# A scan layer and mixture of experts on one core: a new order of every engine's list within a chunk, and of the transfers

## The chip, the core and the metric

The kernel runs on one core of a Trainium2 chip. A core has five engines that run their own lists in order: PE (matmuls; its weight loads are shown as PEld), DVE (vector), ACT (scalar), POOL (GpSimd) and SP, whose queue issues most DMAs here. They meet only through semaphores. The metric is the device time in microseconds; smaller is better.

## The reference

One layer of an adaptively modulated block, on x of 4 sequences x 2048 tokens x 256 channels, all in float32:

```
x = x + ga * attn(layernorm(x) * (1 + ca) + sa)
x = x + gb * moe (layernorm(x) * (1 + cb) + sb)

attn: xs, res = split(x @ in_proj.T)                  # 512 channels each
      xs = silu(causal conv of 4 taps(xs) + conv_b)
      dt, B, C = split(xs @ x_proj.T)                 # 64, 16, 16
      delta = softplus(dt @ dt_proj.T + b);  A = -exp(A_log)
      h = exp(delta * A) * h + delta * xs * B         # over the tokens, 512 x 16 states
      y = sum over the 16 states of h * C
      out = (y * silu(res)) @ out_proj.T
moe:  one shared expert for all tokens, and of seven others the best one for each token,
      each silu(b) * a with a, b = split(x @ w1), then @ w2
```

## The kernel before

The first of its two programs does the attention, the shared expert and the routing; the second gathers tokens for the seven other experts. The change touches only tables of the first.

The 8192 tokens are 16 chunks of 512, four to a sequence. In a chunk the 512 x 16 states are 16 **sets** of 32 channels, a set has 4 **groups** of 4 states, and a group is one tile of 128 partitions x 512 tokens. (s, g) is group g of set s; 64 scans make a chunk. Each set s passes through these steps:

- SP copies delta of 32 channels to four blocks of partitions (transfer `D` s). ACT makes dA = exp(delta * a) for each group (`exps`, L850) into three banks of PSUM, so it can be three scans ahead of DVE.
- The input delta * xs is spread over the partitions, for ten sets by PE (`spread_u`, L580, called U here) and then multiplied by B on DVE (L960, a load of a set into the ring of 8 sets), for the six sets 2, 5, 7, 10, 13 and 15 by a DMA (transfer `U` s) and multiplied by B on POOL (`IN` s, L1272).
- DVE scans the four groups (L973). ACT saves the last column as the state (`save`, L865); the save of set s-1 stands just ahead of dA (s, 3) in ACT's list.
- POOL multiplies the set by C (`weigh_states`, L1279, the weighing), PE adds up the states of four sets (`SUM` j, L590, sets 4j to 4j+3), and DVE multiplies that by the gate (L982). Only when SUM j is made may a set take the ring's places that its sets held.

Between these stand the items of the rest of the layer. Their **names**: `T`, `XS`, `RS`, `CV`, `XP`, `DT`, `DB` are the front of a later chunk (turning, input projection, convolution, x_proj, delta and its linear branch), `OP` the output projection, `T2`, `RB`, `GL`, `GT`, `B`, `A`, `Y` the shared expert of an earlier chunk (turned norm, rows back for the routing, logits, logits turned, the two halves of w1, w2). `LN`, `LN2` are layer norms on DVE, `R`, `R2` their reciprocal roots on POOL, `N`, `N2` the normalizing on ACT, `G`, `G0`, `GM`, `RC` the shared expert's gate, `DU` delta * xs on POOL, `L0`, `L1` the logarithms, `SU` and `SRS` the silus with the loads of their tables (L753, L757, L761, L764), `HALO` three columns of the convolution. An item carries an offset: ("XS", 0), 1 in chunk c works for chunk c+1.

What **sets the order** are tables: `plan[s]` lists what PE does in set s after its U, `evict[s][g]` what ACT does after dA (s, g), `vector[s][g]` what DVE does after scan (s, g), `gps[s]` what POOL does after the weighing of set s, and `transfers` SP's list for a chunk. Each list is followed strictly in order, and an item blocks all behind it on its engine until its semaphores are there. Items that ACT evicts from PSUM share two banks in turn, items that DVE reads (SUM, OP, DB, A, Y) share one; `take_bank` makes PE wait until the item before in the bank is evicted. Chunks 0, 1, 14 and 15 are written out, the others are four to a round of a loop.

Of the kernel before, what the change touches and what calls it, by code (L numbers as in the profile page):

```python
# [102 lines left out]
def fused_program(nc, ins, t, bc_dram, wout_dram, w2_dram, mod_dram, gb_dram, rows_dram, logits_dram):  # L103
# [5 lines left out]
    with ExitStack() as ctx:  # L109
# [78 lines left out]
        plan = {
            0: [(('Y', 1), -2), (('XS', 0), 1), (('XS', 1), 1), (('DB', 2), 0), (('XS', 2), 1), (('DB', 3), 0), (('XS', 3), 1)],
            1: [],  # L190
            2: [(('SUM', 3), -1)],
            3: [(('CV', 0), 1), (('CV', 1), 1)],
            4: [],
            5: [(('OP', 0), -1), (('CV', 2), 1), (('CV', 3), 1), (('OP', 1), -1), (('RS', 0), 1), (('RS', 1), 1), (('SUM', 0), 0), (('XP', 0), 1)],
            6: [],
            7: [],
            8: [(('RS', 2), 1), (('RS', 3), 1), (('T2', 0), -1), (('T2', 1), -1), (('DT', 0), 1), (('DT', 1), 1), (('RB', 0), -1)],
            9: [(('GL', 0), -1), (('RB', 1), -1), (('SUM', 1), 0), (('GT', 0), -1), (('B', 0), -1), (('B', 1), -1), (('B', 2), -1), (('DB', 0), 1), (('B', 3), -1), (('DT', 2), 1)],
            10: [],
            11: [(('DB', 1), 1), (('DT', 3), 1), (('A', 0), -1)],  # L200
            12: [(('T', 0), 2), (('SUM', 2), 0), (('T', 1), 2)],
            13: [(('A', 1), -1), (('A', 2), -1)],
            14: [(('A', 3), -1)],
            15: [(('Y', 0), -1)]}
        evict = {
# [16 lines left out]
        vector = {  # L222
            0: [[(('Y', 1), -2)], [], [(('DB', 2), 0)], []],
            1: [[], [(('DB', 3), 0)], [], []],
            2: [[], [], [], []],
            3: [[(('SUM', 3), -1)], [], [], []],
            4: [[], [], [], [(('OP', 0), -1)]],
            5: [[], [], [], [(('OP', 1), -1)]],
            6: [[(('LN2', 0), -1)], [], [], []],
            7: [[], [(('SUM', 0), 0)], [], []],  # L230
            8: [[], [], [], []],
            9: [[], [], [], []],
            10: [[], [(('SUM', 1), 0), (('LN', 0), 2)], [], []],
            11: [[], [], [(('DB', 0), 1)], []],
            12: [[(('DB', 1), 1)], [], [], [(('A', 0), -1), (('RC', 0), -1)]],
            13: [[], [], [(('SUM', 2), 0)], []],
            14: [[(('RC', 1), -1), (('A', 1), -1)], [], [(('A', 2), -1)], []],
            15: [[(('A', 3), -1)], [], [], [(('Y', 0), -1)]]}
        gps = {
            0: [(('DU', 1), 0), (('IN', 5), 0)],  # L240
            1: [],
            2: [],
            3: [(('IN', 7), 0)],
            4: [(('R2', 0), -1)],
            5: [(('IN', 10), 0)],
            6: [],
            7: [],
            8: [(('IN', 13), 0), (('R', 0), 2), (('G0', 0), -1)],
            9: [],
            10: [],  # L250
            11: [(('IN', 15), 0), (('DU', 0), 1)],
            12: [],
            13: [],
            14: [(('IN', 2), 1)],
            15: []}
# [1365 lines left out]
```

How the kernel before makes its waits and increments, by code:

```python
def hold(eng, sem, value, held):  # L63
    eng.wait_ge(sem, value)
    eng.sem_inc(held, 1)
# [235 lines left out]
        def take_bank(pe, g, c, f):  # L303
            at = (c, g, f) if known(c) else (2, g, 2 + off_of_item[g])
            if at in before:
                x, b = before[at]
                pe.wait_ge(kept[x[0]], many[x[0]] * (b if known(c) else c + (b - 2)) + x[1] + 1)
            return banks[bank_of[g]]
# [1 line left out]
        def read_bank(eng, g, f):  # L311
            eng.wait_ge(made[g[0]], many[g[0]] * f + g[1] + 1)
            return banks[bank_of[g]]
# [22 lines left out]
            def keep_bc(f):  # L336
                sp.wait_ge(xdbl_ready, f + 1)
                sp.dma_start(bc_dram, xdbl[DT_ROWS:PROJ, :]).then_inc(bc_kept, 16)
# [7 lines left out]
            def spread_bc(f, par):  # L346
                keep_bc(f)
                hold(sp, bc_kept, 16 * f + 16, held)
                if known(f) and f == 1:
                    sp.wait_ge(scaled, 2 * BATCH)
                if not known(f) or f >= 2:
                    sp.wait_ge(dbu_own, N_OWN * (f - 1))
                    sp.wait_ge(dbu_shared, N_SHARED * (f - 1))
                load_rep(b_rep, 0, par, b_loaded)
                if not known(f) or f >= 2:
                    sp.wait_ge(hc_ready, NSET * (f - 1))
                load_rep(c_rep, 1, par, crep_loaded)
# [72 lines left out]
            def body(c, m):  # L431
# [5 lines left out]
                    transfer(kind, n, c, m)  # L437
                    if known(c) and c == 0 and kind == "X":
                        sp.wait_ge(ga_stored, 16)
                        load_w_out(0)
```

## Time and profile before

| | us |
|---|---|
| median of 3 runs | 2424.81 (2423.86 to 2426.68) |
| profiled execution | 2425.52 |
| its span, first to last instruction | 2423.7 |
| its mean granted clock of TensorE | 0.917 of 2.4 GHz |
| POOL's first step of the root `R` in four chunks in a row | 1051.67, 1167.04, 1283.50, 1399.13 |

The chunks take the span's first 1890 us; then come the last routing and the experts. In the profile a busy time is the time in which an engine runs instructions; idle time stands in brackets ahead of an instruction, with the engine and line that ended it. A chunk here is counted from one `R` to the next, so it begins in set 9 of one chunk and ends in set 8 of the following. The first chunk of a sequence scans without a start state, and each such scan is a little shorter.

### The profile page before, as it was taken

What the parts mean: (1) busy time and instruction counts of PE and PEld (TensorE: products, weight loads), DVE (VectorE), ACT (ScalarE), POOL (GpSimd) and SP (SyncE); (2) the same over time, 40 slices, a digit from 0 to 9 for tenths busy, and PEclk for the clock granted to TensorE, in tenths of its full rate; (3) what the DMA queues carried; (4) which work ended last, traced back from release to release, by engine and by line L of the source; (5) the groups of instructions that cost most, each with busy time, mean ns of one, the idle gap of its engine ahead of it and who ended that gap; (6) DMA issues with size and microseconds to landing.
All of it is one profiled execution on the core that took longest, in us unless ns stands there. A gap on an engine that the chain in (4) does not pass through costs nothing. (4 is left out here: it accounts for less than half of the span.)

```text
span 2423.7 us, 31216 instructions
## 1 busy us (share of the span) xinstructions
PE 2129.3 (88%) x7668; PEld 1007.6 (42%) x7669; DVE 1948.4 (80%) x2114; ACT 1346.9 (56%) x2391; POOL 1979.4 (82%) x858
## 2 busy tenths in 40 slices
...
GB/s 175 137 101 98 78 106 65 104 74 117 77 102 72 98 74 103 83 101 103 75 111 74 108 68 117 80 103 69 98 69 53 208 42 87 86 87 85 84 85 47
DMA packets 148360, 224.35 MB, mean 93 GB/s; under 512 B 47187, under 2 KB 84577, under 8 KB 144098
## 3 DMA queue, kind: packets, MB, share of 16 engines
...
q14 instruction: 109, 0.89, 0.1%
...
## 5 line engine op out<-in xcount | busy, mean ns | idle before, releaser
L1279 POOL TENSOR_TENSOR ring<-ring,reps 128x2048 f32<-128x2048 f32 x256 | 1154.7, 4530 | 42.6 <-ACT state L865 42.6
L973 DVE TENSOR_TENSOR_SCAN ring<-dA,state,ring 128x512 f32<-128x512 f32 x768 | 929.7, 1262 | 13.5 <-ACT dA L850 9.2
L850 ACT ACTIVATE dA<-d_rep,a 128x512 f32<-128x512 f32 x1024 | 690.1, 686 | 433.1 <-DVE ring L973 426.4
L1272 POOL TENSOR_TENSOR ring<-u_rep,reps 128x2048 f32<-128x2048 f32 x96 | 436.2, 4544 | 44.6 <-PE bank L590 44.5
L960 DVE TENSOR_TENSOR ring<-u_ps,reps 128x2048 f32<-128x2048 f32 x160 | 360.5, 2269 | 8.8 <-issue 4.9
L590 PE MATMUL bank<-ring,spread 128*32 128x512 f32 x2048 | 283.2, 703 | 42.4 <-POOL ring L1279 37.8
L561 PE MATMUL bank<-n,w1s 128*128 128x512 f32 x512 | 266.1, 657 | 61.1 <-DVE delta L941 38.5
L973 DVE TENSOR_TENSOR_SCAN ring<-dA,ring 128x512 f32<-128x512 f32 x256 | 293.7, 1201 | 11.5 <-ACT dA L850 10.4
L1553 DVE TENSOR_TENSOR hid<-z,sg 128x512 f32<-128x512 f32 x70 | 48.4, 692 | 295.6 <-ACT sg L1530 295.6
L1468 PE MATMUL z<-ring,hT 128*128 x560 | 262.2, 612 | 3.6 <-issue 2.1
L516 PE MATMUL bank<-xin,w_in 128*128 128x512 f32 x512 | 244.9, 619 | 8.3 <-ACT xin L701 8.3
L520 PE MATMUL bank<-xpad,w_conv 128*128 128x512 f32 x496 | 224.0, 601 | 8.9 <-ACT us L716 8.8
L527 PE MATMUL bank<-xdbl,w_dt 65*128 65x512 f32 x256 | 149.0, 680 | 68.9 <-ACT n L732 52.1
...
L561 PEld LDWEIGHTS bank<-n,w1s 128*128 128x128 f32 x512 | 98.2, 205 | 195.6 <-issue 93.2
L590 PEld LDWEIGHTS bank<-ring,spread 128*32 128x32 f32 x2048 | 69.9, 127 | 233.4 <-issue 213.2
L580 PE MATMUL u_ps<-us,spread 32*128 32x512 f32 x320 | 161.6, 705 | 0.0
L516 PEld LDWEIGHTS bank<-xin,w_in 128*128 128x128 f32 x512 | 99.6, 198 | 131.9 <-issue 119.2
L1468 PEld LDWEIGHTS z<-ring,hT 128*128 128x128 f32 x560 | 101.9, 192 | 122.4 <-issue 122.3
L1530 ACT ACTIVATE sg<-z 128x512 f32<-128x512 f32 x70 | 41.8, 597 | 199.5 <-PE z L1468 199.5
L520 PEld LDWEIGHTS bank<-xpad,w_conv 128*128 128x128 f32 x496 | 92.1, 190 | 132.5 <-issue 110.8
L1486 PE MATMUL y_ps<-reps,hidT 128*128 x560 | 132.4, 379 | 0.8 <-ACT hidT L1519 0.8
...
## 6 DMA issues: line engine op xcount, KB each, us to landing
d_rep<-delta SPq DMA_DIRECT2D x1024, 64.0 KB, 2.0
reps<-bc_rows SPq DMA_DIRECT2D x128, 256.0 KB, 6.3
u_rep<-us SPq DMA_DIRECT2D x384, 64.0 KB, 2.0
...
```

Of the source, the lines that this page charges most:

```text
L516: last = nc.tensor.matmul(ps_[:, :], t["w_in"][:, k, col:col + P], hT[:, k, :], start=(k == 0), stop=(k == KD - 1))
L520: last = nc.tensor.matmul(ps_[:, :], t["w_conv"][:, j, k, :], xpad[:, j, k:k + T], start=(k == 0), stop=(k == KCONV - 1))
L527: last = nc.tensor.matmul(ps_[:, :], t["w_dt"][:, j * P:(j + 1) * P], xdbl[0:DT_ROWS, :], start=True, stop=True)
L561: last = nc.tensor.matmul(ps_[:, :], t["w1s"][:, k, col:col + P], h2T[:, k, :], start=(k == 0), stop=(k == KD - 1))
L580: nc.tensor.matmul(u_ps[:, i % 2, :], t["spread"][DS * q:DS * q + DS].rearrange("p f d -> p (f d)"), us[DS * q:DS * q + DS, par, j, :], st ...
L590: last = nc.tensor.matmul(ps_[DS * q:DS * q + DS, :], t["gather"], hs[:, (SPC * j + q) % RING, n, :], start=(n == 0), stop=(n == NG - 1), ...
L850: nc.scalar.activation(dA[:, u % ABANK, :], d_rep[:, q, :], ACT.Exp, scale=t["a"][:, u:u + 1]).then_inc(da_ready, 1)
L960: nc.vector.tensor_tensor(hs[:, s % RING], u_ps[:, i % 2, :].unsqueeze(1).to_broadcast([P, NG, T]), b_rep[:, par, :].rearrange("p (g t) -> ...
L973: nc.vector.tensor_tensor_scan(hs[:, s % RING, g, :], dA[:, u % ABANK, :], hs[:, s % RING, g, :], state[:, u:u + 1] if m else 0.0, ALU.mul ...
L1272: nc.gpsimd.tensor_tensor(hs[:, s % RING], u_rep[:, i % UBUF, :].unsqueeze(1).to_broadcast([P, NG, T]), b_rep[:, par, :].rearrange("p (g t ...
L1279: nc.gpsimd.tensor_tensor(hs[:, s % RING, :, :], hs[:, s % RING, :, :], c_rep[:, par, :].rearrange("p (g t) -> p g t", g=NG), ALU.mult).th ...
L1468: last = nc.tensor.matmul(z[:, q % 2, half, :], hT[:, q % 2, i, :], t["w1r"][:, e, i, half * H:(half + 1) * H], start=(i == 0), stop=(i == ...
```

## The change

`plan`, `evict`, `vector`, `gps` and `transfers` get new contents, each with the same items and the same offsets, in other places and partly in another order. Two of the lines that say most (the table `evict` ahead, `vector` behind), and the ends of POOL's and SP's lists:

```diff
-            10: [[(('GL', 0), -1), (('L0', 0), 1), (('RB', 1), -1)], [], [(('GT', 0), -1), (('B', 0), -1)], [(('B', 1), -1)]],
+            10: [[(('L0', 0), 1)], [(('RB', 1), -1), (('GL', 0), -1)], [(('GT', 0), -1)], []],
+            11: [[], [(('B', 0), -1)], [(('B', 1), -1)], [(('B', 2), -1)]],
...
-            10: [[], [(('SUM', 1), 0), (('LN', 0), 2)], [], []],
+            11: [[], [], [(('SUM', 1), 0)], [(('LN', 0), 2), (('DB', 0), 1)]],
...
-            8: [(('IN', 13), 0), (('R', 0), 2), (('G0', 0), -1)],
+            9: [(('G0', 0), -1), (('IN', 13), 0)],
+            10: [(('R', 0), 2)],
...
-                     ('U', 13), ('D', 10), ('D', 9), ('BC', 0), ('X', 0), ('D', 11), ('ROWS', 0), ('D', 12), ('D', 13), ('D', 15), ('D', 14), ('LOG', 0),
-                     ('U', 15), ('D1', 0), ('U1', 2), ('D1', 2), ('D1', 1), ('D1', 3)]
+                     ('D', 11), ('X', 0), ('ROWS', 0), ('D', 12), ('U', 15), ('D', 15), ('D', 14), ('LOG', 0), ('D', 13), ('D1', 0), ('D1', 1), ('D1', 2), ('D1', 3), ('WO', 0), ('U1', 2)]
```

All line numbers of the changed kernel are one smaller from the transfers on. The pieces below are from chunk 1, which is written out; the loop has the same order.

**DVE, sets 6 to 12.** Before. L982 is the gate of SUM, L916 and L922 the layer norm, L960 a load, L973 a scan, L941 DB:

```order
L973 SCALAR_TENSOR_TENSOR ring<-dA,state,ring 128x512 x5
L982 TENSOR_TENSOR res<-bank,res 128x512
L973 SCALAR_TENSOR_TENSOR ring<-dA,state,ring 128x512 x2
L960 TENSOR_TENSOR ring<-u_ps,reps 128x2048 x2
L973 SCALAR_TENSOR_TENSOR ring<-dA,state,ring 128x512 x8
L960 TENSOR_TENSOR ring<-u_ps,reps 128x2048
L973 SCALAR_TENSOR_TENSOR ring<-dA,state,ring 128x512 x2
L982 TENSOR_TENSOR res<-bank,res 128x512
L916 BN_STATS stats<-xin 128x6 x4
L922 BN_AGGR mv<-stats 128x2 x4
L973 SCALAR_TENSOR_TENSOR ring<-dA,state,ring 128x512 x5
L941 SCALAR_TENSOR_TENSOR delta<-delta,bank 128x512
```

Now, from behind LN2 to DB 0 (L981 is the gate, L972 a scan):

```order
L972 SCALAR_TENSOR_TENSOR ring<-dA,state,ring 128x512 x6
L959 TENSOR_TENSOR ring<-u_ps,reps 128x2048 x2
L972 SCALAR_TENSOR_TENSOR ring<-dA,state,ring 128x512 x3
L981 TENSOR_TENSOR res<-bank,res 128x512
L972 SCALAR_TENSOR_TENSOR ring<-dA,state,ring 128x512 x5
L959 TENSOR_TENSOR ring<-u_ps,reps 128x2048
L972 SCALAR_TENSOR_TENSOR ring<-dA,state,ring 128x512 x7
L981 TENSOR_TENSOR res<-bank,res 128x512
L972 SCALAR_TENSOR_TENSOR ring<-dA,state,ring 128x512
L915 BN_STATS stats<-xin 128x6 x4
L921 BN_AGGR mv<-stats 128x2 x4
L940 SCALAR_TENSOR_TENSOR delta<-delta,bank 128x512
```

The gates of SUM 0 and SUM 1 stand five scans later, and the norm stands six scans later, behind SUM 1 by one scan and directly ahead of DB 0.

**ACT, around the logits.** Before. L735 evicts RB, L737 GL, L741 GT, L745 B, L749 is L0, L865 saves a state:

```order
L737 ACTIVATE xpad<-bank 128x128
L749 ACTIVATE delta<-delta 128x1024
L735 ACTIVATE xpad<-bank 128x512
L850 ACTIVATE dA<-d_rep,a 128x512 x2
L741 ACTIVATE lg<-bank 128x32
L745 ACTIVATE xpad<-bank 128x512
L865 ACTIVATE state<-ring 128x4
L850 ACTIVATE dA<-d_rep,a 128x512
```

Now (each line one less):

```order
L748 ACTIVATE delta<-delta 128x1024
L849 ACTIVATE dA<-d_rep,a 128x512
L734 ACTIVATE xpad<-bank 128x512
L736 ACTIVATE xpad<-bank 128x128
L849 ACTIVATE dA<-d_rep,a 128x512
L740 ACTIVATE lg<-bank 128x32
L864 ACTIVATE state<-ring 128x4
L849 ACTIVATE dA<-d_rep,a 128x512 x3
L744 ACTIVATE xpad<-bank 128x512
```

GT still stands ahead of state 9 and dA (10, 3); the first B has moved from between them to behind dA (10, 3), (11, 0) and (11, 1).

**POOL, sets 6 to 12.** Before. L1279 is a weighing, L1272 a load, L1235 to L1240 the root R, L1260 the gate's first step:

```order
L1279 TENSOR_TENSOR ring<-ring,reps 128x2048 x3
L1272 TENSOR_TENSOR ring<-u_rep,reps 128x2048
L1235 TENSOR_SCALAR mv<-mv 128x4
L1236 TENSOR_SCALAR mv<-mv 128x4
L1238 TENSOR_TENSOR rstd<-mv,mhalf 128x4
L1240 TENSOR_TENSOR shift<-mv,rstd 128x4
L1260 TENSOR_TENSOR gs<-lg 128x4
L1279 TENSOR_TENSOR ring<-ring,reps 128x2048 x3
```

Now:

```order
L1278 TENSOR_TENSOR ring<-ring,reps 128x2048 x3
L1259 TENSOR_TENSOR gs<-lg 128x4
L1271 TENSOR_TENSOR ring<-u_rep,reps 128x2048
L1278 TENSOR_TENSOR ring<-ring,reps 128x2048
L1234 TENSOR_SCALAR mv<-mv 128x4
L1235 TENSOR_SCALAR mv<-mv 128x4
L1237 TENSOR_TENSOR rstd<-mv,mhalf 128x4
L1239 TENSOR_TENSOR shift<-mv,rstd 128x4
```

The three weighings ahead of the load of set 13 are now those of sets 7 to 9 instead of 6 to 8, and the root comes behind set 10's.

## Rows read from the trace of the kernel before

**Rows 1.** The page, section 1: busy us, share, instructions by engine

```profile
PE 2129.3 (88%) x7668; PEld 1007.6 (42%) x7669; DVE 1948.4 (80%) x2114; ACT 1346.9 (56%) x2391; POOL 1979.4 (82%) x858
```

**Rows 2.** Busy us by stretch: PE, PEld, DVE, ACT, POOL; then clock, DMA

```profile
1167.04:1283.50 116.46, 103.85 (x374) 45.23 (x373) 111.31 (x111) 77.35 (x137) 107.20 (x34) 0.91 0.35 88
...
938.66:1399.13 460.47, 415.13 (x1493) 179.74 (x1492) 441.39 (x441) 308.67 (x545) 428.82 (x132) 0.91 0.36 91
```

**Rows 3.** Waits of DVE over four chunks: total us, times, longest

```profile
DVE res L982 <- PE bank L590: 8.5, 7, 1.7
DVE ring L973 <- ACT dA L850: 2.6, 4, 0.9
DVE ring L960 <- issue: 2.4, 1, 2.4
```

**Rows 4.** Timeline of DVE: start, us, line, operation, count, idle before and releaser

```profile
1264.06 9.49 DVE L973 TENSOR_TENSOR_SCAN ring<-dA,state,ring 128x512 f32<-128x512 f32 x8
...
1278.83 0.69 DVE L982 TENSOR_TENSOR res<-bank,res 128x512 f32<-128x512 f32 x1 [0.73 <-PE bank L590]
...
1281.11 0.38 DVE L922 BATCH_NORM_AGGREGATE mv<-stats 128x2 f32<-128x6 f32 x4 [0.27 <-DVE stats L916]
```

**Rows 5.** Timeline of PE in the same chunk

```profile
1176.97 3.78 PE L561 MATMUL bank<-n,w1s 128*128 128x512 f32 x4 [2.86 <-DVE delta L941]
...
1219.03 3.64 PE L590 MATMUL bank<-ring,spread 128*32 128x512 f32 x32
...
1262.95 1.12 PE L527 MATMUL bank<-xdbl,w_dt 65*128 65x512 f32 x2 [1.09 <-ACT n L732]
1266.81 2.08 PE L527 MATMUL bank<-xdbl,w_dt 65*128 65x512 f32 x2 [2.73 <-ACT n L732]
1268.67 1.06 PE L547 MATMUL bank<-ident,n 128*128 128x128 f32 x4
1269.66 2.07 PE L580 MATMUL u_ps<-us,spread 32*128 32x512 f32 x2
1271.66 1.04 PE L552 MATMUL bank<-n,wg 128*8 128x128 f32 x16
...
1273.68 5.07 PE L590 MATMUL bank<-ring,spread 128*32 128x512 f32 x32
```

**Rows 6.** Busy us by stretch, the granted clock the third number from the end

```profile
1259.04:1266.04 7.00, 3.69 (x14) 1.59 (x12) 7.00 (x5) 4.24 (x9) 7.00 (x2) 1.00 0.75 175
1267.04:1275.04 8.00, 8.00 (x36) 3.15 (x40) 8.00 (x7) 6.70 (x14) 8.00 (x2) 0.50 0.81 187
```

**Rows 7.** Timeline of ACT in the same chunk

```profile
1265.99 0.76 ACT L732 ACTIVATE n<-bank,sb,cb 128x512 f32<-128x512 f32 x1
...
1279.05 0.20 ACT L741 ACTIVATE lg<-bank 128x32 f32<-128x32 f32 x1 [3.38 <-PE bank L556]
1280.77 0.60 ACT L745 ACTIVATE xpad<-bank 128x512 f32<-128x512 f32 x1 [1.52 <-PE bank L561]
...
1281.37 0.69 ACT L850 ACTIVATE dA<-d_rep,a 128x512 f32<-128x512 f32 x1
```

**Rows 8.** Timeline of DVE in the chunk before the last

```profile
1735.66 0.69 DVE L982 TENSOR_TENSOR res<-bank,res 128x512 f32<-128x512 f32 x1 [1.28 <-PE bank L590]
...
1738.91 1.28 DVE L973 TENSOR_TENSOR_SCAN ring<-dA,state,ring 128x512 f32<-128x512 f32 x1 [1.36 <-ACT dA L850]
```

**Rows 9.** Timeline of POOL, load of set 13

```profile
1278.88 4.54 POOL L1272 TENSOR_TENSOR ring<-u_rep,reps 128x2048 f32<-128x2048 f32 x1 [3.16 <-PE bank L590]
```

**Rows 10.** Timeline of ACT, first eviction of a chunk

```profile
1207.65 0.60 ACT L706 ACTIVATE xpad<-bank 128x512 f32<-128x512 f32 x1 [4.84 <-PE bank L516]
```

**Rows 11.** Timeline of DVE around set 12

```profile
1178.69 2.46 DVE L973 TENSOR_TENSOR_SCAN ring<-dA,state,ring 128x512 f32<-128x512 f32 x2 [0.57 <-ACT dA L850]
...
1182.01 2.29 DVE L960 TENSOR_TENSOR ring<-u_ps,reps 128x2048 f32<-128x2048 f32 x1 [0.20 <-PE u_ps L580]
```

**Rows 12.** The page, section 6: transfer, count, KB each, median us to landing

```profile
d_rep<-delta SPq DMA_DIRECT2D x1024, 64.0 KB, 2.0
```

More of the change, by code:

```diff
@@ L188, in fused_program @@
         plan = {
[L189 to L204, printed above, removed]
-        evict = {
[16 rows of a table removed]
-        vector = {
[L223 to L231, printed above, removed]
+            0: [(('Y', 1), -2), (('XS', 0), 1), (('XS', 1), 1), (('XS', 2), 1), (('DB', 2), 0)],
@@ new lines, in fused_program @@
+            1: [(('XS', 3), 1), (('DB', 3), 0)],
+            2: [(('SUM', 3), -1), (('CV', 0), 1), (('CV', 1), 1), (('OP', 0), -1)],
+            3: [(('CV', 2), 1)],
+            4: [(('CV', 3), 1), (('RS', 0), 1)],
+            5: [(('OP', 1), -1), (('RS', 1), 1)],
+            6: [(('SUM', 0), 0), (('XP', 0), 1)],
+            7: [(('RS', 2), 1)],
+            8: [(('RS', 3), 1), (('T2', 0), -1), (('T2', 1), -1), (('DT', 0), 1), (('DT', 1), 1), (('RB', 0), -1), (('RB', 1), -1)],
+            9: [(('GL', 0), -1), (('SUM', 1), 0), (('GT', 0), -1), (('B', 0), -1), (('B', 1), -1), (('B', 2), -1), (('B', 3), -1)],
@@ new lines, in fused_program @@
+            10: [(('DB', 0), 1), (('DB', 1), 1)],
+            11: [(('DT', 2), 1), (('A', 0), -1)],
+            12: [(('DT', 3), 1), (('SUM', 2), 0), (('T', 0), 2), (('A', 1), -1)],
+            13: [(('T', 1), 2), (('A', 2), -1), (('A', 3), -1)],
+            14: [(('Y', 0), -1)],
+            15: []}
+        evict = {
[16 rows of a table added]
+        vector = {
+            0: [[], [(('Y', 1), -2)], [], []],
+            1: [[(('DB', 2), 0)], [], [(('DB', 3), 0)], []],
+            2: [[], [], [], [(('SUM', 3), -1)]],
+            3: [[], [], [], []],
+            4: [[], [(('OP', 0), -1)], [], []],
+            5: [[], [], [], []],
+            6: [[(('OP', 1), -1)], [(('LN2', 0), -1)], [], []],
+            7: [[], [], [], []],
+            8: [[], [], [(('SUM', 0), 0)], []],
@@ L232, in fused_program @@
             9: [[], [], [], []],
-            10: [[], [(('SUM', 1), 0), (('LN', 0), 2)], [], []],
-            11: [[], [], [(('DB', 0), 1)], []],
+            10: [[], [], [], []],
+            11: [[], [], [(('SUM', 1), 0)], [(('LN', 0), 2), (('DB', 0), 1)]],
             12: [[(('DB', 1), 1)], [], [], [(('A', 0), -1), (('RC', 0), -1)]],
             13: [[], [], [(('SUM', 2), 0)], []],
-            14: [[(('RC', 1), -1), (('A', 1), -1)], [], [(('A', 2), -1)], []],
+            14: [[(('A', 1), -1)], [], [(('RC', 1), -1), (('A', 2), -1)], []],
@@ L238, in fused_program @@
             15: [[(('A', 3), -1)], [], [], [(('Y', 0), -1)]]}
         gps = {
-            0: [(('DU', 1), 0), (('IN', 5), 0)],
+            0: [(('IN', 5), 0), (('IN', 7), 0)],
             1: [],
             2: [],
[L243 to L246, printed above, removed]
+            3: [(('DU', 1), 0)],
+            4: [],
+            5: [(('R2', 0), -1)],
+            6: [(('IN', 10), 0)],
             7: [],
-            8: [(('IN', 13), 0), (('R', 0), 2), (('G0', 0), -1)],
```

9 lines of the change are left out of this document (4 added, 5 removed), and 29 rows, old and new, of the table evict.

## The prediction, written before the changed kernel was run

> **What bounds the kernel now.** I read the page first, then the busy times by chunk, then the waits of each engine over four steady chunks, then the timelines around the longest of them. On the page no engine is free: PE is busy 88% of the span, POOL 82%, DVE 80% [rows 1], but these are means over the chunks and an expert stage that the change doesn't touch. The chunks say more. One of them (1167.04 to 1283.50) takes 116.46 us, with DVE busy 111.31, POOL 107.20 and PE 103.85; four in a row take 460.47 us with 441.39 of DVE [rows 2]. So DVE sets the pace: a chunk is 110.3 us of its work plus 4.8 us in which it stands still, and only these 4.8 can be won or enlarged by an order, since no operation goes. POOL has 7.9 us of slack in a chunk, ACT much more.
>
> DVE's waits tell what the 4.8 us are [rows 3]. Of 19.1 us in four chunks, 8.5 (7 times) go to PE's sums of the states (SUM), 2.6 to dA from ACT, 2.4 once to the head of the loop ("issue"); the other 5.6 are short ones beside Y, the norms and the loads. SUM 1 is late in each of the four chunks and SUM 2 in three, the longest by 1.7; with 1.5 for each SUM 2, (8.5 - 4.5)/4 = 1.0 is left for SUM 1, and 0.73 stands in the chunk shown [rows 4].
>
> Why is SUM 1 late? PE waits twice for ACT's eviction of a turned norm (T2), 1.09 and 2.73 us, and then runs DT, RB, U, GL, RB and SUM 1 in a row for 12 us [rows 5], the first 8 or more at half clock: 0.50 of 2.4 GHz, that is 1.2 GHz, where it was 1.00 ahead of the gaps [rows 6]. Behind SUM 1 comes the turning of the logits (GT). ACT waits for that 3.38 us, and the next dA stands behind it in ACT's list [rows 7]. DVE doesn't feel this today, because it gates SUM 1 and does the layer norm exactly there [rows 4].
>
> **The change, part by part.** (s, g) is the scan of set s, group g; a scan is 1.19 us (9.49 for 8 [rows 4]).
>
> *DVE's gates.* SUM 1 is gated at (11, 2) instead of (10, 1), five scans or 6 us later. Its wait goes: -1.0 a chunk. SUM 0 goes from (7, 1) to (8, 2), SUM 3 from (3, 0) to (2, 3), one scan earlier. PE can start SUM 3 when DVE has taken DB 3 at (1, 2): one U of about 1.1 and 3.64 of SUM [rows 5] against a load and five scans, some 8 us, on DVE. No wait.
>
> *The cover that goes with it.* At (10, 1) gate and norm kept DVE busy from 1278.83 to 1281.49 [rows 4] while ACT got past GT. The norm is now at (11, 3), and DVE runs set 10 without a break; it needs dA (10, 3), which is behind GT in ACT's list. I count from e, the end of scan (8, 0), on which ACT's T2 hangs in both orders; in the chunk shown e is 1264.06 + 1.19 = 1265.25, and SUM 1 starts 8.4 later. After the change, dA and T2 0 on ACT take 0.69 + 0.76 [rows 7]; then PE has DT 0 behind this wait as well: DT 1.12, DT 2.08, two RB 1.06 each, U 2.07, GL 1.04 [rows 5]. The sum is e + 9.9; each pair of PE rows overlaps by 0.1, so e + 9.5. SUM 1 starts 1.1 later than now and has less of itself under the slow clock: 4.5 instead of 5.07. GT 0.3; then on ACT 0.20, a state of 0.20 and dA 0.69 [rows 7]: e + 15.3. DVE gets there after 10 scans, the gate of SUM 0 and a load of 2.2: e + 14.7. A wait of 0.6. Bounds: 0 if PE is at full clock from e on (DT, U, GL and SUM 1 are then 4 us shorter), 2.0 if SUM 1 stays slow. The nearest row is in the chunk that has no next norm to do: DVE waited 1.28 for SUM 1 and 1.36 more for this dA [rows 8]. There, as in the chunk shown, an eviction of B that was waited for 1.52 [rows 7] stood between GT and dA; the new list has B behind two dA more. I take +0.6.
>
> *POOL.* Its load of set 13 stood one weighing behind the one that completes SUM 1's input and waited 3.16 for SUM 1 [rows 9]; it now stands two behind, and the wait goes. But the weighing of set 9 now comes before it, and needs the state that ACT saves behind GT: about 2 us of wait. The loads of sets 5 and 7 both follow set 0's weighing, and set 5's needs SUM 3, which PE reaches only when DVE has taken DB 3: I expect a wait of some 3 us. POOL has 107.2 + 2 + 3 + 1 = 113 us in a chunk of 115. It costs nothing, unless set 11's weighing comes later and with it SUM 2; gain and loss cancel there within 1 us. SUM 2's wait (1.1 a chunk now): I take 0 of change, between -1.1 and +1.
>
> *ACT.* XS 0's eviction, which ACT waited for 4.84 us with the state of set 15 behind it [rows 10], now follows that state. Set 15's weighing can start 5 us earlier; POOL had filled this time with set 2's load, which now comes after it. 0 on DVE. The pair of silus with its table loads at (12, 1) cost DVE 0.57 for dA and then 0.20 for U [rows 11]. The norm at (11, 3) covers the first, but DVE is then earlier at U, which stands behind A 0 on PE: A 0 starts at 1176.97, after 2.86 us of waiting for DVE's DB 1, and runs 3.78 slow [rows 5]; DVE's load behind U started at 1182.01, 5.0 later. Without the two waits DVE would be there 4.3 after that start. So 0.8 stays in another place: 0.
>
> *Transfers.* SP's part of a chunk now ends with D 15, D 14, LOG, D 13. D 15 may go when set 11's dA is done; with three sets to issue from there and 2.0 us to land [rows 12], D 13 arrives when ACT wants it, and ACT is 4 us ahead of DVE there. U 13 and U 10 wait for DU 1, which is later on POOL, and are wanted 8 us after it. 0; a late D 13 would cost under 1.
>
> **Sum.** -1.0 + 0.6 = -0.4 on DVE in each of 14 chunks: -6. In the last two, which have no next norm, 1.28 + 1.36 are lost today and I leave them half: -1.3 each, -3. In the start and in the tail the items keep their order but for RB 1 before GL and A 1 before a reciprocal: within 1. Together some -9. The profiled execution took 2425.5 us (1.8 beyond its span), 0.7 above the median of 2424.8: 2425.5 - 0.7 - 9.5 is 2415.
>
> [...]
>
> **Rivals.** *The clock stays up.* In the new order PE has one wait at T2 instead of two, and a dense stretch from Y 1 to SUM 3. If that keeps it at 2.4 GHz in sets 8 to 13, there is no stall at dA, A 0 (3.78) takes under 2 and lets U go, and SUM 2 is in time: -1.0 - 0.8 - 1.1 = -2.9 a chunk, 14 times -41, 2384. Against it: T2's wait is still 2 us, and so is that between DB 1 and A 0.
> *An even exchange.* The stall at dA is as long as the wait that went, 1.0: 0 a chunk, 2420 to 2428. For it: it is the same chain of T2, SUM 1 and GT, under a shorter cover.
> *Slower: GT holds the scans.* If SUM 1 takes half a us more than 5.07 and starts half a us later than I count, dA (10, 3) comes 2.0 late, POOL's set 9 is 3 us late, and set 11's weighing with nothing left to make it up delays SUM 2 by 0.5: -1.0 + 2.0 + 0.5 = +1.5 at most, 14 times +21: 2430 to 2446. It decides from where GT is made later than e + 15. For it: [rows 8]. Against: B is no longer between.
> *POOL becomes the bound.* If SUM 3 comes 3 us later than I count, set 5's load waits 6 and POOL's chunk is 116: 2435. Against: PE has hardly a gap there.
>
> **How the numbers follow.** Chances: forecast 0.40 (2405 to 2420), clock 0.17, even exchange 0.20, GT 0.18, POOL 0.05. A measurement of this kernel can tell 0.2%, 4.9 us, from no change. Faster: nearly all of the forecast and the clock, 0.54. Slower: GT and POOL, 0.22. Same: 0.24. The range takes the forecast, the even exchange, most of GT and a part of the clock: 2389 to 2438.
>
> **What would show it.** In the new profile DVE's waits for SUM fall from 8.5 to about 4.5 in four chunks, and those for dA rise from 2.6 to between 3 and 5, at the fourth scan of set 10; ACT still waits 3 us for GT; POOL waits some 3 us for SUM early in a chunk and no longer in its middle; DVE's busy time stays at 441. I am wrong if no wait for dA stands at set 10 (the clock's case), if it is over 1.5 (GT's), or if DVE waits for POOL's loads.

## The result, and the profile after

| | before | after |
|---|---|---|
| median | 2424.79 us (2423.86 to 2426.68) | 2443.05 us (2435.46 to 2447.32, 4 runs) |
| ratio to before | | 1.0072, interval [1.0049, 1.0094] |
| profiled execution, span, clock | 2425.52, 2423.7, 0.917 | 2435.46, 2433.7, 0.912 |

The change made the kernel slower by 0.7%. The forecast was 2415, and the range ended at 2438. The executions lie further apart than those of before: 12 us against 3.

In what follows chunks are counted from 0 and (s, g) is a scan, as in the prediction. Where a chunk's duration is given, it is counted from its scan (0, 0) to the next chunk's. The loop's rounds begin with chunks 2, 6 and 10. All lines of the changed kernel are one smaller.

The page's first section, which answers [rows 1]:

```profile
PE 2172.4 (89%) x7668; PEld 1016.7 (42%) x7669; DVE 1954.6 (80%) x2114; ACT 1348.3 (55%) x2391; POOL 1980.2 (81%) x858
```

The same instructions took PE 43 us longer and DVE 6.2 longer. Of PE's 43 us, 39 are booked on U (161.6 to 200.6 us in the list by lines); the mean clock fell only from 0.917 to 0.912, so half clock alone doesn't explain them, and it isn't shown what does. The busy times of four chunks in a row, from one R to the next, answer [rows 2] (columns as there):

```profile
956.51:1417.28 460.77, 423.04 (x1492) 181.91 (x1492) 442.55 (x441) 308.90 (x545) 428.74 (x133) 0.92 0.36 91
```

Four steady chunks take 460.77 against 460.47: no gain, no loss. DVE's waits over four chunks answer [rows 3], POOL's stand behind them:

```profile
DVE ring L972 <- ACT dA L849: 5.3, 6, 1.9
...
DVE ring L959 <- PE u_ps L579: 2.0, 4, 0.6
DVE res L981 <- PE bank L589: 1.5, 1, 1.5
...
DVE xpad L995 <- PE bank L560: 1.2, 3, 0.5
```

```profile
POOL ring L1278 <- ACT state L864: 15.7, 8, 4.1
POOL ring L1271 <- PE bank L589: 11.7, 4, 3.1
```

The wait for SUM fell from 8.5 to 1.5, further than to the 4.5 expected. dA rose from 2.6 to 5.3, and U and A 0, which cost next to nothing before, now cost 3.2. The new stall stands where it was put, at (10, 3). DVE, then PE and ACT in chunk 7 answer [rows 4, 5, 7]:

```profile
943.21 4.81 DVE L972 TENSOR_TENSOR_SCAN ring<-dA,state,ring 128x512 f32<-128x512 f32 x4 [1.91 <-ACT dA L849]
```

```profile
927.84 3.78 PE L526 MATMUL bank<-xdbl,w_dt 65*128 65x512 f32 x4 [2.40 <-ACT n L731]
...
936.17 5.82 PE L589 MATMUL bank<-ring,spread 128*32 128x512 f32 x32
...
963.21 3.64 PE L589 MATMUL bank<-ring,spread 128*32 128x512 f32 x32 [0.32 <-POOL ring L1278]
```

```profile
942.29 0.20 ACT L740 ACTIVATE lg<-bank 128x32 f32<-128x32 f32 x1 [3.92 <-PE bank L555]
```

PE waits 2.40 for T2 and then runs DT to SUM 1 at half clock; SUM 1 takes 5.82 where 4.5 was counted. ACT waits for GT, and DVE for the dA behind it. POOL waits for the state behind it too (4.09 in this chunk), and DVE waits nowhere for POOL.

The last of PE's lines is SUM 2, and it says what became of its wait. In the kernel before, SUM 2 ran at half clock, as in chunk 10:

```profile
1300.00 5.34 PE L590 MATMUL bank<-ring,spread 128*32 128x512 f32 x32 [0.83 <-POOL ring L1279]
```

It took 5.1 to 5.4 us in ten of its chunks 1 to 13, and DVE waited for it in these; it took 3.64 in the other three (3, 9 and 11), without a wait. After the change it takes 3.64 in ten and 5.24 in three (5, 9 and 13), and only these three have the wait, of 1.5. So the half clock now covers all or nearly all of SUM 1 in most chunks, and no longer SUM 2.

**What nobody priced: the loop's heads.** Chunk 6 took 121.42 us, chunk 10, with the same list, 114.58 (columns as above; the clock is the third number from the end):

```profile
748.89:870.31 121.42, 110.37 (x368) 45.86 (x368) 111.67 (x111) 77.75 (x136) 103.89 (x33) 0.86 0.34 85
1216.46:1331.04 114.58, 102.63 (x368) 44.20 (x368) 111.36 (x112) 77.33 (x136) 104.13 (x33) 0.93 0.36 90
```

PE at the head of chunk 6, then DVE, then the busy times there:

```profile
751.45 2.40 PE L515 MATMUL bank<-xin,w_in 128*128 128x512 f32 x4 [2.24 <-ACT xpad L705]
...
764.91 6.12 PE L589 MATMUL bank<-ring,spread 128*32 128x512 f32 x32
```

```profile
744.48 4.49 DVE L959 TENSOR_TENSOR ring<-u_ps,reps 128x2048 f32<-128x2048 f32 x2 [2.55 <-issue]
...
763.02 0.69 DVE L940 SCALAR_TENSOR_TENSOR delta<-delta,bank 128x512 f32<-128x512 f32 x1 [4.26 <-PE bank L526]
```

```profile
752.00:760.00 8.00, 8.00 (x11) 2.67 (x10) 6.70 (x7) 4.64 (x9) 4.44 (x2) 0.56 0.44 131
```

At the turn of the loop DVE stands still for 2.55 us ("issue"; before has this too). ACT's dA (0, 3) waits for DVE's scan (0, 0), and XS 0's eviction now stands behind that dA. So PE, which has made XS 0 and XS 1 into its two banks, waits 2.24 for the first. Its clock goes from 1.00 to 0.56 and 0.50, 1.2 GHz, SUM 3 takes 6.12, and DVE waits 4.26 for DB 3. At the head of chunk 10 the gap is 2.19 and nothing follows. In the steady chunks PE has no gap there: in chunk 7 it makes XS 0 to XS 2 in a row in 5.31 us.

The kernel before also hands this stall to PE, in another place: ahead of DB 2, whose bank DVE empties when it takes Y 1. In its other steady chunks PE has no gap there either. Its heads of chunks 6 and 10:

```profile
751.78 1.13 PE L527 MATMUL bank<-xdbl,w_dt 65*128 65x512 f32 x2 [1.79 <-DVE xres L1011]
...
1210.93 1.28 PE L527 MATMUL bank<-xdbl,w_dt 65*128 65x512 f32 x2 [1.60 <-DVE xres L1011]
1212.00 3.47 PE L516 MATMUL bank<-xin,w_in 128*128 128x512 f32 x4
```

Behind the first of these gaps nothing follows. Behind the second, one XS runs at half clock (3.47 for 1.88), the next item is back at full clock, and DVE loses nothing. So PE stood still at the head before, too; what is new is where, and that a fall of the clock there can cost something. In the profiles of the kernel before and of runs 7, 11 and 12, which have its order, the clock fell at four of eight heads and DVE lost nothing at any. In those of the changed kernel and of runs 1, 4, 6, 13 and 14 it fell at seven of twelve: five cost DVE 1.2 us at DB 2 and DB 3, two (the one above, and chunk 10 in run 14) cost 6.1 and 6.0 at DB 3, U and the item behind.

### The profile page after: what moved, and what is told of

Its sections match the earlier page's. It is cut to its first block and busy times, and to the rows that moved or that the text cites. A ratio compares the mean times of both kernels' runs of the same rounds, so it can differ in the third digit from the quotient of the medians.

```text
span 2433.7 us, 31216 instructions
## 1 busy us (share of the span) xinstructions
PE 2172.4 (89%) x7668; PEld 1016.7 (42%) x7669; DVE 1954.6 (80%) x2114; ACT 1348.3 (55%) x2391; POOL 1980.2 (81%) x858
## 5 line engine op out<-in xcount | busy, mean ns | idle before, releaser
L972 DVE TENSOR_TENSOR_SCAN ring<-dA,state,ring 128x512 f32<-128x512 f32 x768 | 930.9, 1265 | 22.2 <-ACT dA L849 17.7
L589 PE MATMUL bank<-ring,spread 128*32 128x512 f32 x2048 | 277.0, 689 | 36.4 <-POOL ring L1278 34.2
L972 DVE TENSOR_TENSOR_SCAN ring<-dA,ring 128x512 f32<-128x512 f32 x256 | 294.4, 1204 | 15.7 <-ACT dA L849 14.8
L526 PE MATMUL bank<-xdbl,w_dt 65*128 65x512 f32 x256 | 162.6, 746 | 53.9 <-ACT n L731 29.1
L579 PE MATMUL u_ps<-us,spread 32*128 32x512 f32 x320 | 200.6, 716 | 7.8 <-POOL us L1245 7.8
```

Source lines behind the costliest of these rows:

```text
L579: nc.tensor.matmul(u_ps[:, i % 2, :], t["spread"][DS * q:DS * q + DS].rearrange("p f d -> p (f d)"), us[DS * q:DS * q + DS, par, j, :], st ...
L589: last = nc.tensor.matmul(ps_[DS * q:DS * q + DS, :], t["gather"], hs[:, (SPC * j + q) % RING, n, :], start=(n == 0), stop=(n == NG - 1), ...
L972: nc.vector.tensor_tensor_scan(hs[:, s % RING, g, :], dA[:, u % ABANK, :], hs[:, s % RING, g, :], state[:, u:u + 1] if m else 0.0, ALU.mul ...
```

## The experiments

Ratios are to the kernel before. A row of `evict` or `vector` is one set, with four lists, one for each scan.

**1. The changed kernel once more.**

> The changed kernel itself, unaltered, for the spread of its runs and a second profile. Theory H (head): at the head of each round of the loop (chunks 2, 6, 10, 14) DVE loses 2.5 us, PE waits 2.2 us for the eviction of XS 0, and in some executions this gap puts PE's clock to its half for about 15 us, which costs some 7 us each time. The first profile had it once (2435.5), so runs should lie at steps of 5 to 7 us: 2428, 2435, 2442, 2449, and a second profile should show XS 2, U, DB 3 and SUM 3 at twice their time in one to four of the four heads. Rival D (drift): the loss is spread over all chunks by the stall at dA (10, 3), and the run-to-run spread is noise: then a slower profile shows about the same first 20 us in all chunks, and longer waits at set 10.

2438.59 (2428.03 to 2441.75), ratio 1.0057 [1.0039, 1.0074]. The six values are 2428.0, 2428.8, 2436.2, 2441.0, 2441.4 and 2441.8. The profiled execution (2428.81) has neither head slow. Its PE at the head of chunk 6:

```profile
751.49 1.98 PE L515 MATMUL bank<-xin,w_in 128*128 128x512 f32 x4 [2.10 <-ACT xpad L705]
...
759.35 3.64 PE L589 MATMUL bank<-ring,spread 128*32 128x512 f32 x32
```

The gap is as long, the clock stays up, and chunk 6 takes 114.61, which is 6.8 less. The values fit none, one or two slow heads of about 6.7 us each; only executions with a profile show how many. The highest value of the first measurement, 2447.3, is 5 above two heads, and is not explained by this.

**2. XS 1 made twice at the heads (chunks 2, 6, 10 and 14).**

```diff
+                    for rep in range(2 if g == ("XS", 1) and off == 1 and par == 0 and head[0] else 1):
                         for k in range(KD):
```

> As the changed kernel, but PE makes XS 1 twice at the head of each round of the loop (the same result; 1.8 us more of PE's work, inside its 2.2 us gap before XS 2). Theory H: the gap shrinks to 0.4 us, the clock stays at 2.4 GHz there in every execution, the time falls to 2426 to 2431 and its spread to under 4 us. Rival D: no change of the median (2443), or 1 us more for each head, since PE has more to do.

2435.61 (2434.14 to 2441.12), ratio 1.0056 [1.0043, 1.0069]. Chunks 6 and 10 took 114.5 and 114.6. But chunk 14, which has no turn of the loop and no gap to fill, took 119.05 where it had taken 113.73: the repeat pushed DB 2 and DB 3 back by 0.5 and 0.8, and SUM 1 and SUM 2 ran slower behind it (clock of the chunk 0.89 for 0.92). Chunk 2 has no gap there either and got the same repeat, and took 116.11 where it had taken 116.03. So a fill without a gap can cost as much as the gap, or nothing.

**3. XS 0 evicted one scan earlier.**

```diff
-            0: [[], [], [], [(('XS', 0), 1)]],
+            0: [[], [], [(('XS', 0), 1)], []],
```

> As the changed kernel, but XS 0 is evicted behind dA (0, 2) again, ahead of the state of set 15, as in the kernel before. Theory H: PE doesn't wait for bank 0 at the heads, so no slow stretch: 2426 to 2432, narrow spread. Price: the weighing of set 15 and the load of set 2 on POOL start 5 us later, which DVE doesn't feel (set 2's scan has 8 us of room), so under 1 us a chunk. If the early state is what the new order lives on, the time is over 2450 instead.

2441.27 (2440.32 to 2444.81), ratio 1.0076 [1.0063, 1.0089]. The gap ahead of XS 2 is gone at both heads, so it is the place of XS 0's eviction that makes it. But the time was not won: PE now stands a little later, at DB 2, for DVE to take Y 1. At the head of chunk 10:

```profile
1217.35 1.12 PE L526 MATMUL bank<-xdbl,w_dt 65*128 65x512 f32 x2 [0.96 <-DVE xres L1010]
...
1219.90 3.78 PE L515 MATMUL bank<-xin,w_in 128*128 128x512 f32 x4
```

The clock fell here too, SUM 3 took 6.23, and the chunk 118.85, 4.3 more than in run 1; chunks 4, 8 and 12 took 1.7 to 2.5 more. This moves the heads' gap and doesn't mend them.

**4. GT evicted behind dA (10, 3).**

```diff
-            10: [[(('L0', 0), 1)], [(('RB', 1), -1), (('GL', 0), -1)], [(('GT', 0), -1)], []],
+            10: [[(('L0', 0), 1)], [(('RB', 1), -1), (('GL', 0), -1)], [], [(('GT', 0), -1)]],
```

> As the changed kernel, but GT is evicted behind dA (10, 3) instead of ahead of it. If the stall of 1.4 us at scan (10, 3) in 15 chunks is what ate the 1.0 of SUM 1, it shrinks to under 0.5 and the median falls by 10 to 18 us (2425 to 2433 beside 2443), with the same spread as the changed kernel. If the stall only moves to dA (11, 0), which now stands behind GT, the median falls by under 5.

2434.94 (2430.83 to 2437.94), ratio 1.0046 [1.0033, 1.0059]. This is 3.7 below run 1, which was made beside it, and 8.1 below the first measurement; 10 to 18 were expected. The stall at (10, 3) went, and DVE waits for DB 0 ahead of (12, 0) instead in most chunks. The profile shows what the order alone doesn't decide. Chunks 7 and 9:

```profile
867.95:980.70 112.75, 104.05 (x374) 45.00 (x373) 111.17 (x111) 77.67 (x136) 107.28 (x34) 0.94 0.36 90
1092.44:1213.01 120.57, 112.03 (x380) 47.27 (x378) 111.85 (x112) 77.45 (x136) 110.16 (x35) 0.89 0.35 88
```

```profile
925.47 1.98 PE L526 MATMUL bank<-xdbl,w_dt 65*128 65x512 f32 x4 [2.40 <-ACT n L731]
...
932.32 4.59 PE L589 MATMUL bank<-ring,spread 128*32 128x512 f32 x32
...
1149.95 3.78 PE L526 MATMUL bank<-xdbl,w_dt 65*128 65x512 f32 x4 [2.40 <-ACT n L731]
...
1158.28 5.95 PE L589 MATMUL bank<-ring,spread 128*32 128x512 f32 x32
```

Both have the same gap of 2.40 at T2. Behind one the two DT still run at full clock and SUM 1 takes 4.59; behind the other they run at half and it takes 5.95. The first chunk has no single wait over 0.3 us on DVE, the second loses 0.8, 0.9, 1.2 and 1.7 at (11, 0), DB 0, U and SUM 2. Of chunk 9's 120.57 us, 2.3 are the turn of the loop, which falls into its end by this count; 118.3 against 112.75 are left to compare.

**5. XS 1 twice only in chunks 2, 6 and 10** (`head[0] = m == 2 and not known(c)`, `known(c)` being true of the chunks that are written out).

> The changed kernel with one addition: PE makes item XS 1 twice, only in the two chunks of the loop at whose head DVE stalls for the branch (and the one of the first round), so that it has work where it waits 2.2 us for ACT's eviction of XS 0; the chunks that are written out stay as they are. Theory H (this gap at the head, where the clock falls in some executions, is what makes the time differ by 6 to 7 us a head): 2426 to 2431 in all executions, a spread under 4 us, chunks 6 and 10 at 114.5. Rival N (the levels come from elsewhere, the heads only show them): values still between 2428 and 2442. If the dearer thing is that doubling only moves the fall to a later gap in the same chunk: 2434 to 2436 in all.

2430.57 (2427.36 to 2433.84), ratio 1.0028 [1.0016, 1.004]. The head of chunk 6:

```profile
751.49 1.99 PE L518 MATMUL bank<-xin,w_in 128*128 128x512 f32 x4 [0.43 <-ACT xpad L709]
```

XS 2 starts at 751.49 as in run 1: the repeat made nothing earlier, it only took the place of 1.7 us of the gap. None of the six executions is above 2434, where 8 of the 10 of the changed kernel are above 2435. So the slow heads are what the times above 2434 come from. The spread is 6.5, not under 4; what sets the two groups 2427.4 to 2428.4 and 2432.7 to 2433.8 apart isn't known, since the profile is of the lower one.

**6 to 8. The norm back at (10, 1).** Run 6 changes only this in the changed kernel; run 8 adds the repeat of run 5; run 7 is the kernel before with SUM 1's gate at (11, 0).

```diff
-            10: [[], [], [], []],
-            11: [[], [], [(('SUM', 1), 0)], [(('LN', 0), 2), (('DB', 0), 1)]],
+            10: [[], [(('LN', 0), 2)], [], []],
+            11: [[], [], [(('SUM', 1), 0)], [(('DB', 0), 1)]],
```

```diff
-            10: [[], [(('SUM', 1), 0), (('LN', 0), 2)], [], []],
-            11: [[], [], [(('DB', 0), 1)], []],
+            10: [[], [(('LN', 0), 2)], [], []],
+            11: [[(('SUM', 1), 0)], [], [(('DB', 0), 1)]],
```

> The changed kernel with the layer norm back at (10, 1) on DVE, SUM 1's gate left at (11, 2). Theory C (the norm's 2 us cover GT in ACT's list; without it dA (10, 3) comes 0.5 to 2.0 late, 1.4 on the mean): the wait at (10, 3) goes in 14 chunks, 0.6 of it comes back at dA (12, 2) ahead of the silus: -0.8 x 14 = -11, 2417 for an execution without a fall of the clock at a head, 2417 to 2431 in all. Rival: the slack is taken by PE's slow stretch behind it (SUM 2, U), as when GT was evicted later: 2428 to 2442 as now.

> The kernel before with one item moved: DVE gates SUM 1 behind scan (11, 0) instead of (10, 1), the norm stays at (10, 1). Theory: of the change's gain the wait for SUM 1 (0.9 a chunk) is kept, the norm of 2 us still covers most of GT, and at most 0.3 comes back at dA (10, 3): -0.6 x 14 = -8, 2416; 2412 to 2420. Rival (even exchange under any cover: whatever DVE doesn't wait for SUM 1 it waits for dA behind GT): 2422 to 2427.

> The changed kernel with both mends: XS 1 made twice at the loop's heads, and the norm back at (10, 1). If the two causes are independent, the sum of both: 2415 to 2420 in all executions, below the kernel before. If the cover of GT is worth nothing, 2426 to 2431; if the heads are not mended, a spread over 7 us.

All three fell the other way: 2444.44 (2438.95 to 2446.05), ratio 1.0076 [1.0063, 1.009]; 2459.68 (2453.59 to 2461.71), 1.0142 [1.0126, 1.0158]; 2443.54 (2441.25 to 2444.86), 1.008 [1.0066, 1.0093]. In run 6 the stall at (10, 3) is gone in chunks 1 to 13, and DVE stands at DB 0, 0.7 to 1.9 in each of these chunks, and at U and SUM 2 behind it (1.2, and 1.7 to 2.1, in six of them). PE makes DB 0 behind the four B and U, in part at the slow clock. Chunk 10:

```profile
1303.27 0.69 DVE L940 SCALAR_TENSOR_TENSOR delta<-delta,bank 128x512 f32<-128x512 f32 x1 [1.57 <-PE bank L526]
```

At (11, 3) the norm covered this. It is one cover of 2 us, and PE is late at both places. Run 7 shows what else the gate did at (10, 1). It empties the bank that DB 0 needs. In run 7 the bank is empty three scans later, PE stops in front of DB 0 with B 3 and U behind it, and DVE gets its U 2.40 late (chunk 10):

```profile
1304.22 1.13 PE L527 MATMUL bank<-xdbl,w_dt 65*128 65x512 f32 x2 [1.45 <-DVE res L982]
```

```profile
1310.71 2.29 DVE L960 TENSOR_TENSOR ring<-u_ps,reps 128x2048 f32<-128x2048 f32 x1 [2.40 <-PE u_ps L580]
```

**9 and 10. PE's gaps filled in the changed kernel**, on top of run 5: T2 1 made four times; in run 10 DT 2 three times as well.

```diff
+                    for rep in range(4 if j == 1 else 1):
                         for tt in range(TT):
```

> The changed kernel with XS 1 made twice at the loop's heads, as in the run that held 2427 to 2434, and in every chunk item T2 1 made four times over, so that PE works through most of the 2.3 us in which it waits for ACT's eviction of T2 0 ahead of DT 0. Theory G (that gap makes the half clock under which GL, SUM 1, GT and the four B run, and so the wait at dA (10, 3)): the slow stretch behind it goes, the waits of 1.0 to 2.0 at (10, 3) go: -1.4 x 14 = -20, 2410; the second gap, ahead of A 0, stays with its short slow stretch. Rival (the clock falls at the next short gap, or stays down for what PE did before): the repeats run slow too, 2430 to 2440.

> As the last, and item DT 2 made three times over, so that PE also works through most of the 2.0 to 2.3 us in which A 0 waits for DVE to take DB 1. Theory G: the waits at (13, 0) for A 0 and U (1.0 together) and for SUM 2 go too: -1.0 x 14 = -14 beside the last, 2396; this is also the test of the rival of the prediction that gave 2384 if the clock stays up. Rival: 2430 or more.

Run 9: 2431.60 (2424.27 to 2436.72), ratio 1.0024 [1.0011, 1.0036]. The stall at (10, 3) is gone in chunks 1 to 14, and in ten of them SUM 1 takes 3.64, at full clock (4.6 to 5.3 in the other four). Nothing is won: in 8 of these chunks DVE now waits 1.2 for U at (13, 0) and 2.0 to 2.3 for SUM 2. The slow stretch has moved behind the next gap, ahead of A 0, and SUM 2 takes 5.92 where it took 3.64 (chunk 7, DVE and PE):

```profile
955.59 2.29 DVE L965 TENSOR_TENSOR ring<-u_ps,reps 128x2048 f32<-128x2048 f32 x1 [1.23 <-PE u_ps L584]
...
963.49 0.69 DVE L987 TENSOR_TENSOR res<-bank,res 128x512 f32<-128x512 f32 x1 [2.07 <-PE bank L594]
```

```profile
945.50 3.78 PE L530 MATMUL bank<-xdbl,w_dt 65*128 65x512 f32 x4 [1.98 <-DVE delta L946]
...
957.49 5.92 PE L594 MATMUL bank<-ring,spread 128*32 128x512 f32 x32
```

This is the rival of run 9's expectation, the fall at the next gap.

Run 10: 2436.90 (2434.45 to 2441.37), 1.0054 [1.0041, 1.0067]. The repeats of DT 2 made A 0 late by 1.0 to 2.8, while SUM 2 took 3.64 in eleven of chunks 1 to 14. The clock over the span was 0.930, the highest of all runs, and the time was 6 us over run 5's. A higher clock was worth nothing here, where the fill itself stood in front of what DVE waits for.

**11 and 12. The same in the kernel before:** T2 1 twice and DT 0 three times; in run 12 also DT 2 three times.

```diff
+                    for rep in range({("DT", 0): 3}.get(g, 1)):
```

> The kernel before with T2 1 made twice and DT 0 three times over, to fill its gaps of 1.1 and 2.7 us for T2's evictions. Theory G: the half clock ahead of SUM 1 goes, and with it the wait at SUM 1 of 0.9: -0.9 x 14 = -13, 2412; 2408 to 2416. Rival: DT 1, RB and U come late behind the repeats, at the slow clock: 2425 to 2440.

> As the last, with DT 2 three times over in the gap of 2.9 us ahead of A 0. Theory G: the wait for SUM 2 (1.1 a chunk) goes as well: 2397; 2392 to 2404. If DT 2's repeats push A 0 and U of set 13 back instead: 2412 to 2430.

Run 11: 2420.46 (2414.25 to 2423.87, 11 runs), ratio 0.998 [0.9971, 0.9989]. This is the one version that beats both kernels, by 3.6 us; 8 more were expected. PE and DVE in chunk 7:

```profile
915.97 2.07 PE L528 MATMUL bank<-xdbl,w_dt 65*128 65x512 f32 x2 [0.19 <-ACT n L734]
...
922.84 4.72 PE L592 MATMUL bank<-ring,spread 128*32 128x512 f32 x32
```

```profile
927.64 0.69 DVE L984 TENSOR_TENSOR res<-bank,res 128x512 f32<-128x512 f32 x1 [0.38 <-PE bank L592]
```

The gap of 2.73 [rows 5] is 0.19 here, and SUM 1 still begins at half clock. Its wait is 0.38, against 0.82 in chunk 7 of the kernel before; it is gone in four chunks that had one and has grown from 0.73 to 1.80 in chunk 10. The profiled execution (2414.72) is one of the fastest, and its chunk 0 alone is 3.8 shorter than in the profile before. So where the 3.6 us come from is shown only in part. Run 12: 2427.95 (2425.86 to 2432.37), 1.0019 [1.001, 1.0028]: the wait for SUM 2 is gone in chunks 1 to 14, but as in run 10 the fill ahead of A 0 delays what stands behind it, here U: DVE waits 1.1 to 1.6 for it at (12, 0), and in most chunks 1.2 more at (13, 0).

**13 to 16. One table at a time.** Run 13 is the changed kernel with the old transfers, run 14 with POOL's old table, run 15 with DVE's; run 16 is the kernel before with the new plan and evict alone. The edits are whole tables, those of the change.

> The changed kernel with the list of SP's transfers as before; every other table as changed. Prediction's term: the transfers are worth 0. If so, as the changed kernel, median 2436 to 2443 with its spread of 13 us. Rival (the new list is what brings transfers late into the head, where the clock falls): 2428 to 2431 with a spread under 5. If before's list brings a set's delta too late for the new ACT order: over 2448.

> The changed kernel with POOL's table as before (load of set 13 one weighing behind SUM 1's, root R ahead of it, sets 5's and 7's loads apart). Prediction's term: POOL's places cost DVE 0. If so 2436 to 2443. Since SUM 1 is gated five scans later and POOL's load of set 13 stands ahead of the weighing of set 9 again, POOL waits for SUM 1 about 4 us; if that delays SUM 2, +0.5 a chunk, 2443 to 2450. Rival (POOL's new waits of 3 and 4 us are what costs the 4 us that the heads leave open): 2424 to 2434.

> The changed kernel with DVE's table as before; PE, ACT, POOL and SP as changed. Gate SUM 1 and norm are at (10, 1) again: DVE waits for SUM 1 there, 1.1 later than before the change, about 2 us, but then nothing at dA (10, 3); DB 0 is gated at (11, 2) again, where PE makes it behind all four B: 1.5 us more of wait. 2440 to 2460. Rival (the DVE table is what costs): 2424 or less.

> The kernel before with the changed plan and evict (PE and ACT) alone. If the place of XS 0's eviction behind state 15 and dA (0, 3) is by itself what brings the slow heads: PE's gap of 2.2 us ahead of XS 2 at the heads, and values spread over more than 8 us (before: 5). SUM 1's wait at (10, 1) grows by 1 a chunk: +14, 2435 to 2455. Rival (the heads need the new DVE order as well): a spread under 6 us.

| | median | ratio |
|---|---|---|
| 13 | 2511.22 (2509.84 to 2517.95) | 1.0359 [1.0345, 1.0374] |
| 14 | 2502.23 (2497.39 to 2503.79) | 1.0314 [1.03, 1.0328] |
| 15 | 2509.17 (2500.10 to 2512.57) | 1.0335 [1.0315, 1.0355] |
| 16 | 2493.31 (2492.77 to 2503.59) | 1.0283 [1.0269, 1.0297] |

None of the times named for a theory came. Run 13 fell in its last branch (a late delta, over 2448), in run 16 the gap and the spread were as expected and the median wasn't. One line of each, in this order: ACT's dA (7, 0) waits for a transfer that the old list issues too late; POOL's root R, ahead of three weighings, waits for the norm that now comes six scans later, and SUM 2 is 7.3 late; DVE, back at (11, 2), wants DB 0 when PE has it behind four B; and PE has the gap at the head of chunk 6 with DVE's old order too:

```profile
949.92 0.69 ACT L850 ACTIVATE dA<-d_rep,a 128x512 f32<-128x512 f32 x1 [6.66 <-DMA d_rep<-delta]
```

```profile
980.03 0.23 POOL L1234 TENSOR_SCALAR mv<-mv 128x4 f32<-128x4 f32 x1 [5.58 <-DVE mv L921]
```

```profile
993.01 0.69 DVE L940 SCALAR_TENSOR_TENSOR delta<-delta,bank 128x512 f32<-128x512 f32 x1 [2.54 <-PE bank L526]
```

```profile
773.72 3.65 PE L516 MATMUL bank<-xin,w_in 128*128 128x512 f32 x4 [2.19 <-ACT xpad L706]
```

So the gap ahead of XS 2 comes from plan and evict alone. It isn't what costs run 16 its 69 us: there DVE waits 57.5 us in all for the DB items. The 4 us of the steady chunks belong to no single table: taking one back costs 59 to 68 us over the changed kernel, putting PE's and ACT's in alone costs 69 over the one before, and only all five together come near to 0. "Transfers 0" and "POOL 0" agree with run 1's profile, in which no wait of DVE over 0.45 us in chunks 1 to 13 hangs on either, but don't hold for these tables taken by themselves.

## Why the prediction was wrong

Against an execution like the profiled one of before, the forecast was 2416.0. Run 1's profiled execution, without slow heads, took 2428.8, and the median 2443. The miss is 12.8 in the chunks and up to two heads of 6.7, which together make the median.

**The step that failed** is ACT's: the place of XS 0's eviction behind the state was costed at "0 on DVE" from a steady chunk, and two rivals rested on the same view ("a dense stretch from Y 1 to SUM 3", "PE has hardly a gap there"). In a steady chunk that is right. At the turn of the loop DVE loses 2.4 us, which stood in [rows 3] as "issue", and the new order hands this to PE by way of dA (0, 3). I had this row and didn't ask who stands behind it. Runs 3 and 16 show that the gap hangs on this place, and runs 1 and 5 that the slow stretch behind it is what the time above 2434 is. It isn't the only way to a slow head: in run 3 the eviction is back, and a gap of 0.96 at DB 2 did the same.

**The sum.** Without slow heads, idle and busy time of DVE from the first scan to the end of the last, before and in run 1 (columns as in [rows 2]):

```profile
60.47:1888.01 1827.54, 1588.63 (x5683) 682.01 (x5681) 1746.17 (x1714) 1203.14 (x2115) 1713.62 (x520) 0.90 0.35 90
```

```profile
59.90:1891.32 1831.42, 1626.31 (x5681) 690.85 (x5681) 1750.00 (x1714) 1203.77 (x2114) 1711.49 (x519) 0.90 0.35 90
```

DVE stands still for 81.4 us in both, where 9.5 less was forecast; it is busy 3.8 longer, where no change was expected, and starts 0.6 earlier. These three, 9.6 + 3.8 - 0.6, are the 12.8. Of the 3.8, longer loads (2269 to 2274 ns on the mean) and scans (1262 to 1263) give some 2; what makes them longer stays open. DVE's waits from 60 to 1900 us (total, times, longest), before and in run 1:

```profile
DVE res L982 <- PE bank L590: 38.2, 26, 4.9
DVE ring L973 <- ACT dA L850: 19.6, 21, 4.7
...
DVE ring L960 <- PE u_ps L580: 1.0, 4, 0.4
```

```profile
DVE ring L972 <- ACT dA L849: 32.0, 28, 4.6
DVE ring L959 <- PE u_ps L579: 9.7, 16, 1.7
DVE res L981 <- PE bank L589: 9.5, 5, 2.7
...
DVE xpad L995 <- PE bank L560: 4.2, 11, 0.5
...
DVE delta L940 <- PE bank L526: 1.8, 2, 1.5
```

- SUM: -28.7, where about -15 was counted. SUM 1's wait went, but it was worth 10.3 in chunks 1 to 14 and not 14: the four chunks of [rows 3] all have it, and four of the others have none over 0.45. SUM 2's, costed at 0 of change, went in most chunks, since it now runs at full clock: -11.3. The start (chunk 0), costed at "within 1", gave -6.1 here, and 3.3 less idle time in all.
- dA: +12.4, where +0.6 for (10, 3) and -0.57 for the silus made 0. The stall at (10, 3) was 0.49 to 2.02 in run 1's chunks 1 to 13, 1.28 on the mean. The mis-sized part is SUM 1's slow stretch. In chunks 5, 9 and 13 SUM 1 took 4.4 and the stall was 0.5, as counted (4.5 and 0.6), and just there SUM 2 is slow and awaited; in the others SUM 1 took 5.2 to 5.9, up to 1.4 more than counted.
- U and A 0: +12.9, where 0.8 a chunk was said to stay: right in place and nearly in size.
- DB +1.8.
- The last chunk: 3.2 at (10, 3) and 2.4 at SUM 2, where it had lost 2.5 at SUM 2 and 0.8 at dA. The prediction took it to lose 2.6 today as chunk 14 does [rows 8] and to win 1.3. Chunk 14 did win, 2.1.

In short: the sum took one course of the clock for all chunks, up again within SUM 1 and down at SUM 2 as before. Only chunks 5, 9 and 13 went so. In the others the half clock stayed for more of SUM 1 and was over by SUM 2, and gain and loss came out equal.

**The rivals.** "An even exchange" was what happened in the chunks, and had 0.20. "GT holds the scans" has the median in its 2430 to 2446, but by luck: (10, 3) was 1.3 late and not 2.0, SUM 2 was earlier and not later, and the heads made the rest. "The clock stays up" didn't come, and was tested only in part: in run 9 SUM 1 ran at full clock and the fall came at the next gap, and in run 10, where SUM 2 mostly did too, the repeats themselves held up A 0. What a clock that stays up without repeats would be worth, 2384 or not, no run shows. POOL's waits came where they were told, 3.1 early in the chunk (some 3 told) and up to 4.1 ahead of set 9's weighing (about 2 told), and DVE waited for POOL nowhere.

**What stays open:** why the same gap is followed by half clock in one chunk or execution and not in the next, and for how long. Gaps of 1.79 (before), 2.10 and 2.19 had nothing behind them, one of 1.60 (before) a single slow item, one of 0.96 (run 3) and one of 2.24 a long slow stretch. The Trainium skill (TensorE: Matmul & The Clock Gate, "HAM oscillation — how this bites in real kernels") describes a kernel in which every wait between groups of matmuls put the array back to its slow clock; its waits, on DMAs, are longer than these, so it doesn't decide this case. The prediction took the clock as given by the order, and it isn't.
